# Sums kept between rounds are added by Pool, and the rounds are cut anew (one-core graph network)

## The chip, the cores and the metric

The kernel runs on one core of one Trainium2 chip. The number that counts is the device time of one launch in microseconds (us). The other seven cores are idle. Everything that is computed, the sorting of the edges into a count matrix included, happens inside that launch.

## What is computed

A graph network with 12,500 nodes of 64 features and 400,000 edges (src, dst). `src` is the node that receives, `dst` the node whose message is sent.

```python
h = relu(layernorm(x))
for l in range(3):
    mlp = lambda z: relu(z @ W1[l] + b1[l]) @ W2[l] + b2[l]
    msgs = mlp(h[dst])
    agg  = segment_sum(msgs, src, 12500)
    h    = mlp(h + agg)
out = x + h @ Wf + bf
```

Since the message depends on the sending node alone, the kernel computes one message for each node and forms `agg` as a product with a dense matrix of edge counts (12,544 x 12,544, four bits for each count).

## The kernel before, in words

**Counts.** The matrix is built once and kept in DRAM (`counts_dram`) as 98 tiles of 128 senders each. A build loop of 196 groups (`for k in range(BUILD * HG)`, index k, four groups for each pair of tiles) makes it. In a group VectorE (DVE) compares keys with two lists of numbers (`make_hots`, L752: 832 column elements, then 4,096 row elements); Pool multiplies the column half with the weights in place (`weigh`, L627); TensorE forms the counts of 32 columns of the group by 32 small matmuls (L1307, `multiply_group`); ScalarE packs the product (`keep_batch`, L1132); DVE transposes it two groups later (`turn_counts`, L760); and SyncE stores it (L439).

**Layer 0 beside the build.** `agg` is the sum over the 98 tiles of `parts` (messages as two 16-bit halves stacked to 128 columns) times counts, for 7 stretches of 1,792 nodes (SB = 7), each of four PSUM banks of 448 (SBB = 4). As the build goes on, this sum is made in rounds: a round takes 14 finished tiles (two chunks of CK = 7). So there are 7 rounds x 7 stretches = 49 units, and a unit is four banks with 14 matmuls each (L1336). DVE unpacks the counts of a unit in four steps, the low and the high nibbles of two chunks (`unpack_low`, L791; `unpack_high`, L799). Between two rounds a bank's sum is kept in SBUF (`kept_sums`): ScalarE copies it out of PSUM (L1141), and in the next round TensorE puts it back into PSUM with a float32 product with the identity (`add_kept`, L1331) ahead of the 14 matmuls.

One bank goes with each group from k = 32 on: 41 units (`FUSED`, 164 banks) lie inside the build loop. The last 8 units follow it, seven of them being the last round. There, unit by unit, DVE reads the finished sums, scales them and adds the rows of h (`read_sums`, L881 and L882, halves of 64 partitions), and TensorE runs the small network of the stretch before (`mlp_stage`) in between.

**Layers 1 and 2** read all counts again from DRAM, 14 chunks for each stretch (L1438, 28 matmuls for each chunk). They start when the scale of layer 1's messages is known (`find_peak`, Pool's `share_peak`, `make_scale`) and the first `parts` are rewritten.

**What sets the order.** Each engine runs its list in the order written, and semaphores tie the lists together. In a group DVE's list is: column compare, row compare, transposition of group k-2, one unpack step. TensorE's is: 32 small matmuls, (keys of the next pair), the kept sum, 14 matmuls. Pool's is: `weigh(k)`, and in every fourth group an indirect gather (L607).

## Time and profile before

| what | value |
|---|---|
| median of three runs | 2259.04 us (2255.1 to 2259.32) |
| the profiled execution's own time | 2256.61 us |
| its span | 2254.9 us |
| TensorE / DVE / ScalarE / Pool busy | 2096.7 / 1512.7 / 663.7 / 643.7 us |
| share of the span, in the same order | 93% / 67% / 29% / 29% |
| chain that ended last | TensorE 80%, DVE 13%, issue 4%, DMA 2% |
| float32 products of kept sums (L1331) | 83.2 + 83.1 us busy, 336 instructions |

The shares are means over stages that have different limits: a build stage up to about 945 us, the rest of layer 0 up to about 1104 us, and layers 1 and 2 after that. A row of the timeline begins with its start and its duration; an instruction's recorded duration can overlap that of the next one on the same engine, so the time which it takes from its engine is the distance from its start to the next start.

### The profile page before, as it was taken

The page shows a single profiled execution, that of the slowest core. Times are in us where ns is not written, and L with a number is a line of the kernel's source. Part 1 is how long each engine was busy: PE and PEld are TensorE (multiplying, and loading weights), DVE is VectorE, ACT ScalarE, POOL GpSimd, SP SyncE. Part 2 cuts the span into 40 slices and gives each one's busy share as a digit, 9 for nine tenths or more (in the row PEclk, how much of TensorE's full clock was granted, in tenths as well). Part 3 has the DMA queues.
Part 4 walks back from the last instruction along what each step waited for, and adds up shares of the span by engine and source line. Part 5 has one row for each costly group of instructions (what it writes and reads, how often), then busy time and mean ns, then how long its engine had stood idle before and what let it go on. Part 6 is the DMA issues. An engine that isn't in the chain of part 4 may idle for free.

```text
span 2254.9 us, 39446 instructions
## 1 busy us (share of the span) xinstructions
PE 2096.7 (93%) x15866; PEld 1153.6 (51%) x15866; DVE 1512.7 (67%) x1683; ACT 663.7 (29%) x1632; POOL 643.7 (29%) x287
## 2 busy tenths in 40 slices
PE   3566779999999999999997999999999999999998
PEld 3444445555555555545553555555555555555554
DVE  7899999999999999846645434444463443444344
ACT  4885655555555555411200000000010000000000
POOL 3666667777767776500000000000000000000000
PEclk8796999999999999999998999999999999999999
DMA  7256666666666666642343435444444554555552
GB/s 194 71 139 180 178 181 189 182 188 196 190 188 193 185 187 176 186 125 72 122 127 110 146 111 160 151 128 145 143 132 134 157 165 126 169 159 159 145 157 68
DMA packets 332824, 344.46 MB, mean 153 GB/s; under 512 B 21562, under 2 KB 303992, under 8 KB 332184
## 3 DMA queue, kind: packets, MB, share of 16 engines
q1 hardware_dynamic: 327516, 335.59, 50.6%
q0 software_dynamic: 2352, 6.43, 1.1%
q8 instruction: 94, 1.54, 0.3%
q10 hardware_dynamic: 2816, 0.53, 0.2%
q14 instruction: 46, 0.38, 0.0%
HBM read 252.58 MB, written 89.89 MB: 152 GB/s over the span
## 4 chain that ended last, share of the span: by engine, by line
PE 80%; DVE 13%; issue 4%; DMA 2%; SPq 0%; ACT 0%; POOL 0%; DVEq 0%; POOLq 0%
PE ps L1438 46%; PE ps L1336 18%; DVE arena L752 6%; PE ps L1331 5%; PE ps L1307 5%; PE ps L1400 2%; DVE arena L760 2%; PE ps L1392 2%; PE ps L1416 1%; DMA arena<-counts_dram 1%; DVE arena L791 1%; DVE arena L799 1%; DVE arena L725 1%; SPq L439 0%; DVE msg L778 0%
## 5 line engine op out<-in xcount | busy, mean ns | idle before, releaser
L1438 PE MATMUL ps<-arena,parts 128*128 128x448 fp8e4 x5488 | 1054.0, 353 | 11.9 <-DVE arena L882 11.9
L1438 PEld LDWEIGHTS ps<-arena,parts 128*128 128x128 f16 x5488 | 535.1, 98 | 531.4 <-issue 44.7
L627 POOL TENSOR_TENSOR arena<-arena,weight_now 128x416 int32<-128x416 int32 x196 | 540.8, 2759 | 274.0 <-DVE arena L752 273.3
L866 DVE TENSOR_SCALAR arena<-arena 128x3136 uint16<-128x3136 uint16 x196 | 191.5, 977 | 624.5 <-PE ps L1438 617.9
L1336 PE MATMUL ps<-arena,parts 128*128 128x448 fp8e4 x2744 | 554.9, 353 | 1.5 <-DVE parts L832 1.5
L752 DVE TENSOR_TENSOR arena<-row_iota,key_now 128x4096 f16<-128x4096 f16 x196 | 446.3, 2277 | 0.0
L1336 PEld LDWEIGHTS ps<-arena,parts 128*128 128x128 f16 x2744 | 267.1, 98 | 296.9 <-issue 83.1
L1132 ACT ACTIVATE arena<-ps 128x800 uint16<-128x800 f32 x392 | 332.3, 874 | 73.2 <-PE ps L1307 64.1
L1200 ACT ACTIVATE arena<-ps,b1s 128x448 f32<-128x448 f32 x42 | 26.6, 634 | 943.5 <-PE ps L1392 943.5
L1307 PE MATMUL ps<-arena 128*128 128x53 fp8e4 x6272 | 204.3, 189 | 79.8 <-DVE arena L752 41.2
L1307 PEld LDWEIGHTS ps<-arena 128*128 128x128 f16 x6272 | 187.7, 98 | 151.4 <-DVE arena L752 95.5
L619 POOL COPY hT<-arena 128x896 f32 (+1 forms) x14 | 13.2, 945 | 699.5 <-ACT arena L1209 699.5
L760 DVE STREAM_TRANSPOSE arena<-arena 128x800 int32<-128x800 int32 x196 | 195.2, 996 | 3.7 <-DMA counts_dram<-arena 3.7
L867 DVE TENSOR_SCALAR arena<-arena 128x3136 uint16<-128x3136 uint16 x196 | 190.0, 969 | 0.0
L647 POOL PARTITION_ALL_REDUCE good<-good x1 | 0.4, 409 | 526.8 <-DVE good L1000 526.8
L752 DVE TENSOR_TENSOR arena<-word_iota,key_now 128x832 uint16<-128x832 f16 x196 | 113.5, 579 | 4.6 <-ACT weight_now L1111 4.6
L1141 ACT ACTIVATE msg<-ps 128x448 f32<-128x448 f32 x84 | 45.7, 544 | 163.7 <-PE ps L1336 163.7
L1331 PE MATMUL ps<-msg,ident 128*128 128x448 f32 x168 | 83.2, 577 | 3.0 <-DVE arena L851 3.0
L1331 PE MATMUL ps<-arena,ident 128*128 128x448 f32 x168 | 83.1, 576 | 0.0
L1141 ACT ACTIVATE arena<-ps 128x448 f32<-128x448 f32 x84 | 45.7, 544 | 118.9 <-PE ps L1336 118.9
L607 POOL DMA_INDIRECT arena<-edges_dram,start_i x49 | 76.5, 1562 | 8.0 <-issue 3.5
L791 DVE TENSOR_SCALAR arena<-arena 128x3136 uint16<-128x3136 uint16 x82 | 76.2, 930 | 3.1 <-DMA arena<-counts_dram 3.0
(127 smaller groups left out, 1146.9 us busy)
## 6 DMA issues: line engine op xcount, KB each, us to landing
arena<-counts_dram SPq DMA_DIRECT2D x294, 784.0 KB, 4.6
counts_dram<-arena SPq DMA_DIRECT2D x784, 100.0 KB, 2.2
h_dram<-parts SPq DMA_DIRECT2D x2, 1536.0 KB, 7.2
edges_dram<-arena SPq DMA_DIRECT2D x2, 1400.0 KB
arena<-in_x_dram SPq DMA_DIRECT2D x14, 192.0 KB
out_dram<-arena SPq DMA_DIRECT2D x14, 192.0 KB
arena<-in_dst_dram SPq DMA_DIRECT2D x1, 1400.0 KB
arena<-in_src_dram SPq DMA_DIRECT2D x1, 1400.0 KB
```

The source lines that it names most:

```text
L627: nc.gpsimd.tensor_tensor(pairs, pairs, weight_now[:, h * HW:(h + 1) * HW].unsqueeze(2).to_broadcast([P, HW, WORDS // 2]), ALU.mult).then_ ...
L752: return v.tensor_tensor(out, numbers.rearrange("p (m two) -> p m two", two=2).unsqueeze(1).to_broadcast(shape), key.unsqueeze(2).to_broad ...
L760: v.transpose(ctile[:, k % 2, :].bitcast(I32), stage[:, k % 2, :].bitcast(I32)).then_inc(s["counts_turned"], 1)
L791: v.tensor_scalar(spread[:, n % WIDE, 0, :].bitcast(U16), ring0[:, n % RING0, :].bitcast(U16), 0x0F0F, None, ALU.bitwise_and).then_inc(s[" ...
L866: v.tensor_scalar(spread[:, c % WIDE, 0, :].bitcast(U16), packed, 0x0F0F, None, ALU.bitwise_and)
L867: v.tensor_scalar(spread[:, c % WIDE, 1, :].bitcast(U16), packed, 4, 0x0F0F, ALU.logical_shift_right, ALU.bitwise_and).then_inc(s["counts_ ...
L1132: a.activation(to, product(q)[:, :, 0:2 * LP].rearrange("p c (m two) -> p c m two", two=2), ACT.Copy, scale=1.0 / WEIGHT_UNIT)
L1141: a.activation(kept_sums(u % SB, b), ps[:, bank, 0:NB], ACT.Copy).then_inc(s["sums_kept"], 1)
L1307: last = t.matmul(product(q)[:, c, 0:COLS], hot_r[:, slot, w, :], hot_c8[:, slot, w, 0:COLS], start=True, stop=True)
L1331: t.matmul(ps[:, bank, 0:NB], ident[:], kept_sums(u % SB, b), start=True, stop=False)
L1336: last = t.matmul(ps[:, bank, 0:NB], parts[:, (ROUND * (u // SB) + c) * CK + k, :], spread[:, c, b // 2, at:at + NB].bitcast(F8), start=u ...
L1438: last = t.matmul(ps[:, b, 0:NB], parts[:, c * CK + k, :], spread[:, c % WIDE, b // 2, at:at + NB].bitcast(F8), start=start, stop=stop)
```

## The change

The kept sums no longer go back through TensorE. In the first round ScalarE copies the bank to `kept_sums`, already scaled; in later rounds it copies the bank, scaled, into one of two stages (`sums_stage`), and Pool adds the stage to `kept_sums` in SBUF (`add_sums`). Pool also adds the rows of h (`add_rows`), once for each of the 28 banks. `read_sums` of layer 0 becomes one operation over 128 partitions instead of two over 64.

There are eight rounds now, of 14, 14, 14, 14, 14, 12, 10 and 6 tiles, so 224 banks ("jobs"). `spread_jobs` gives each job of the first seven rounds the group with which it goes: none, one or two for each group. 179 jobs lie in the build loop, 17 kept ones and the 28 of the last round (six matmuls each) behind it. In the last round each bank is released and refilled by itself, and the steps of the small network go between banks. The scale of layer 1 is taken from the peaks of one stretch fewer and spread by TensorE instead of Pool. ScalarE turns the first keys ahead of the normalisation of the first rows. `row_edges` has 8-bit elements.

```diff
-ROUNDS = CH // ROUND
+COLUMNS = (7, 7, 7, 7, 7, 6, 5, 3)
+ROUNDS = len(COLUMNS)
+FROM = [sum(COLUMNS[:r]) for r in range(ROUNDS + 1)]
 UNITS = ROUNDS * SB
-AHEAD = KG + 1
-FUSED = BUILD - AHEAD
+JOBS = UNITS * SBB
+KEPT = JOBS - SB * SBB
+CREDIT = 16
 RING0 = 3
...
+def spread_jobs():
+    groups, credit = [], 0
+    for k in range(BUILD * HG):
+        credit = 2 * KG if len(groups) < SB * SBB else min(credit, 2 * KG) + CREDIT
+        while len(groups) < KEPT:
+            r = len(groups) // (SB * SBB)
+            if k < HG * (FROM[r + 1] + 1) or credit < 2 * COLUMNS[r]:
+                break
+            credit -= 2 * COLUMNS[r]
+            groups.append(k)
+    return groups + [BUILD * HG] * (JOBS - len(groups))
...
+JOB_GROUP = spread_jobs()
+IN_LOOP = JOB_GROUP.index(BUILD * HG)
+def jobs_with(k):
+    return [n for n in range(IN_LOOP) if JOB_GROUP[n] == k]
+def unpack_group(n):
+    return max(JOB_GROUP[n - 1] if n else 0, JOB_GROUP[n] - 1)
...
-EARLY_PEAKS = {1: 2 * (SB - 2), 2: 2 * (SB - 1)}
+EARLY_PEAKS = {1: 2 * (SB - 3), 2: 2 * (SB - 1)}
-        row_edges = sb("row_edges", [P, BUILD * QN, QW], F16)
+        row_edges = sb("row_edges", [P, BUILD * QN, QW], U8)
+        sums_stage = sb("sums_stage", [P, 2, NB], F32)
...
+            def add_sums(n):
+                pool.wait_ge(s["sums_kept"], n + 1)
+                to = kept_sums(n // SBB % SB, n % SBB)
+                nc.gpsimd.tensor_tensor(to, to, sums_stage[:, n % 2, :], ALU.add).then_inc(s["sums_added"], 1)
+            def add_rows(st, b):
+                own = slice(b // 2 * D, b // 2 * D + D)
+                to = kept_sums(st, b)[own]
+                nc.gpsimd.tensor_tensor(to, to, hT[own, st * SBH + b % 2 * NB:st * SBH + b % 2 * NB + NB],
+                                        ALU.add).then_inc(s["rows_added"], 1)
+            ODD_ROWS = HG * (BUILD - WR + 1)
             for k in range(BUILD * HG):
                 weigh(k)
+                for n in jobs_with(k - 1):
+                    if n >= SB * SBB:
+                        add_sums(n)
+                    elif n % SBB < 2:
+                        pool.wait_ge(s["sums_kept"], n + 1)
+                        add_rows(n // SBB, n % SBB)
+                if 0 <= k - ODD_ROWS < 2 * SB:
+                    n = k - ODD_ROWS
+                    if n == 0:
+                        for r in range(WR):
+                            pool.wait_ge(windows_gathered[r], 16 * len(range(r, WT, WR)))
+                    pool.wait_ge(s["hots_made"], k + 1)
+                    pool.wait_ge(s["sums_added"], max(m for m in jobs_with(k - 1) + [SB * SBB]) + 1 - SB * SBB)
+                    add_rows(n // 2, 2 + n % 2)
+                    pool.wait_ge(s["rows_added"], 2 * SB + n + 1)
                 if k % HG == 2 and k // HG + WR < WT:
                     gather(k // HG + WR)
-            with pool.Fori(0, SB - 2) as i:
+            for n in jobs_with(BUILD * HG - 1):
+                add_sums(n)
+            for n in range(IN_LOOP, KEPT):
+                add_sums(n)
...
+            def unpack_step(n):
+                u, c = n // SBB, n % ROUND
+                m = u * ROUND + c
+                size = tiles_of(u, c)[1] * SBH
+                packed = ring0[:, m % RING0, 0:size].bitcast(U16)
+                if n % SBB < 2:
+                    dve.wait_ge(round_loaded[m % RING0], 16 * (m // RING0 + 1))
+                    if u:
+                        dve.wait_ge(s["sums_done"], SBB * (u - 1) + 2)
+                    v.tensor_scalar(spread[:, c, 0, 0:size].bitcast(U16), packed, 0x0F0F, None, ALU.bitwise_and).then_inc(
+                        s["low_unpacked"], 1)
+                else:
+                    if u:
+                        dve.wait_ge(s["sums_done"], SBB * u)
+                    v.tensor_scalar(spread[:, c, 1, 0:size].bitcast(U16), packed, 4, 0x0F0F, ALU.logical_shift_right,
+                                    ALU.bitwise_and).then_inc(s["counts_unpacked"], 1)
...
+                    if l == 0:
+                        if i == 0 and b == 0:
+                            dve.wait_ge(s["sums_added"], KEPT - SB * SBB)
+                            dve.wait_ge(s["rows_added"], SB * SBB)
+                        if i:
+                            dve.wait_ge(s["u_done"], 2 * (i - 1) + b % 2 + 1)
+                        v.scalar_tensor_tensor(zP[:, b * NB:(b + 1) * NB], ps[:, b, 0:NB], scal[:, 0, 6:7], kept_sums(i, b),
+                                               ALU.mult, ALU.add).then_inc(s["sums_read"], 1)
+                        continue
...
-            act.wait_ge(s["variance_made"], 1)
-            a.activation(stat[:, 2, :], stat[:, 1, :], ACT.Sqrt).then_inc(s["root_made"], 1)
...
             relate_rows(0)
             keep_keys(0, 0)
             keep_keys(0, 1)
+            act.wait_ge(s["variance_made"], 1)
+            a.activation(stat[:, 2, :], stat[:, 1, :], ACT.Sqrt).then_inc(s["root_made"], 1)
+            act.wait_ge(s["norm_made"], 1)
+            make_h0(0)
...
+            def keep_sums(n):
+                u, b = n // SBB, n % SBB
+                act.wait_ge(s["sums_done"], n + 1)
+                if u < SB:
+                    if b < 2:
+                        act.wait_ge(s["parts_made"], ROUND * (u + 1))
+                    to = kept_sums(u, b)
+                else:
+                    if n >= SB * SBB + 2:
+                        act.wait_ge(s["sums_added"], n - 1 - SB * SBB)
+                    to = sums_stage[:, n % 2, :]
+                a.activation(to, ps[:, b % 2, 0:NB], ACT.Copy, scale=scal[:, 0, 6:7]).then_inc(s["sums_kept"], 1)
             def upper_parts(l, n):
...
-            def add_kept(u, b, bank):
-                t.matmul(ps[:, bank, 0:NB], ident[:], kept_sums(u % SB, b), start=True, stop=False)
+            def add_bank(n):
+                u, b = n // SBB, n % SBB
+                bank = b if n >= KEPT else b % 2
+                if n % (SB * SBB) == 0:
+                    pe.wait_ge(s["parts_made"], -(-2 * FROM[u // SB + 1] // CK))
+                if n < 2:
+                    pe.wait_ge(s["hidden0_kept"], BLOCKS)
+                elif n < KEPT:
+                    pe.wait_ge(s["sums_kept"], n - 1)
+                elif n < KEPT + 2:
+                    pe.wait_ge(s["sums_kept"], KEPT)
+                elif n == KEPT + 2:
+                    pe.wait_ge(s["scale_made"], 1)
+                elif n == KEPT + 3:
+                    pe.wait_ge(s["keys_kept"], 2 * BUILD)
                 else:
-                    pe.wait_ge(s["hidden0_kept"], BLOCKS)
-                if u >= SB:
-                    add_kept(u, b, b % 2)
+                    pe.wait_ge(s["sums_read"], n - KEPT - SBB + 1)
                 for c in range(ROUND):
+                    first, tiles = tiles_of(u, c)
                     pe.wait_ge(s["low_unpacked" if b < 2 else "counts_unpacked"], ROUND * u + c + 1)
-                    last = multiply_chunk(u, c, b, b % 2, c == ROUND - 1)
+                    for k in range(tiles):
+                        at = k * SBH + b % 2 * NB
+                        last = t.matmul(ps[:, bank, 0:NB], parts[:, first + k, :], spread[:, c, b // 2, at:at + NB].bitcast(F8),
+                                        start=c == 0 and k == 0, stop=c == ROUND - 1 and k == tiles - 1)
...
+            MLP_AT = ((0, 1), (2,), (3,), (4, 5))
+            for n in range(IN_LOOP, JOBS):
+                add_bank(n)
+                i, b = n // SBB - (UNITS - SB), n % SBB
+                if i >= 1:
+                    for stage_n in MLP_AT[b]:
+                        mlp_stage(0, i - 1, stage_n)
+                if i == SB - 1 and b == 0:
+                    turn_peak(1)
+                if i == SB - 1 and b == 1:
+                    spread_peak(1)
```

The order of Pool's list late in the build loop, before (`weigh` is `arena<-arena,weight_now`, the DMA is the gather):

```order
L627 TENSOR_TENSOR arena<-arena,weight_now 128x32x13 x4
L607 DMA arena<-edges_dram,start_i 128x256
L627 TENSOR_TENSOR arena<-arena,weight_now 128x32x13 x4
L607 DMA arena<-edges_dram,start_i 128x256
L627 TENSOR_TENSOR arena<-arena,weight_now 128x32x13 x4
```

Nothing but the gather stands between the multiplies. And now, at the same place (the new operation reads `sums_stage`; half of the kept sums lie in `msg`, half in `arena`):

```order
L669 TENSOR_TENSOR arena<-arena,weight_now 128x32x13
L679 TENSOR_TENSOR arena<-arena,sums_stage 128x448
L669 TENSOR_TENSOR arena<-arena,weight_now 128x32x13
L679 TENSOR_TENSOR msg<-msg,sums_stage 128x448
L669 TENSOR_TENSOR arena<-arena,weight_now 128x32x13
L679 TENSOR_TENSOR msg<-msg,sums_stage 128x448
L669 TENSOR_TENSOR arena<-arena,weight_now 128x32x13
L679 TENSOR_TENSOR arena<-arena,sums_stage 128x448 x2
L649 DMA arena<-edges_dram,start_i 128x256
L669 TENSOR_TENSOR arena<-arena,weight_now 128x32x13
```

Where four multiplies followed each other between two gathers, an addition of 128x448 stands behind each, in some groups two. In the whole list 148 such additions and 28 of 64x448 (with `hT`) stand ahead of the last multiply, and 20 additions behind it.

DVE's list late in the build loop, before (L760 transposes, L799 and L791 unpack):

```order
L752 TENSOR_TENSOR arena<-word_iota,key_now 128x32x26
L752 TENSOR_TENSOR arena<-row_iota,key_now 128x4096
L760 STREAM_TRANSPOSE arena<-arena 128x800
L799 TENSOR_SCALAR arena<-arena 128x3136
L752 TENSOR_TENSOR arena<-word_iota,key_now 128x32x26
L752 TENSOR_TENSOR arena<-row_iota,key_now 128x4096
L760 STREAM_TRANSPOSE arena<-arena 128x800
L799 TENSOR_SCALAR arena<-arena 128x3136
```

Each group has the same four pieces. And now, two groups of the second to fourth round (L833 transposes, L868 and L873 unpack):

```order
L833 STREAM_TRANSPOSE arena<-arena 128x800
L873 TENSOR_SCALAR arena<-arena 128x3136
L825 TENSOR_TENSOR arena<-word_iota,key_now 128x32x26
L825 TENSOR_TENSOR arena<-row_iota,key_now 128x4096
L833 STREAM_TRANSPOSE arena<-arena 128x800
L873 TENSOR_SCALAR arena<-arena 128x3136
L868 TENSOR_SCALAR arena<-arena 128x3136
```

The pieces of a group are the same; now and then a group has a second unpack step. Ahead of the last row compare stand 164 unpack steps of 3,136 elements before, and 140 of 3,136, 28 of 2,688 and 11 of 2,240 now.

TensorE's list in the last round, one stretch, before (L1331 is the kept sum, L1392, L1400 and L1416 are the small network):

```order
L1336 MATMUL ps<-arena,parts 128x448 x7
L1331 MATMUL ps<-msg,ident 128x448
L1336 MATMUL ps<-arena,parts 128x448 x7
L1392 MATMUL ps<-arena,W1s 64x448 x2
L1331 MATMUL ps<-msg,ident 128x448
L1336 MATMUL ps<-arena,parts 128x448 x7
L1392 MATMUL ps<-arena,W1s 64x448 x2
L1331 MATMUL ps<-arena,ident 128x448
L1336 MATMUL ps<-arena,parts 128x448 x7
L1400 MATMUL ps<-arena,W2b 128x448 x2
L1331 MATMUL ps<-arena,ident 128x448
L1336 MATMUL ps<-arena,parts 128x448 x14
```

Each bank begins with its kept sum, and its 14 matmuls stand in two halves of 7. And now (L1431 is the banks' product; L1477, L1485 and L1501 are the small network):

```order
L1431 MATMUL ps<-arena,parts 128x448 x210
L1477 MATMUL ps<-arena,W1s 64x448 x4
L1431 MATMUL ps<-arena,parts 128x448 x6
L1485 MATMUL ps<-arena,W2b 128x448 x2
L1431 MATMUL ps<-arena,parts 128x448 x6
L1485 MATMUL ps<-arena,W1b 128x448 x2
L1431 MATMUL ps<-arena,parts 128x448 x6
L1501 MATMUL ps<-W2b,arena 128x128 x7
```

The four float32 products of a stretch are gone, and a bank is 6 matmuls where it was 14. The 210 matmuls of the first row are 10 of the build loop's last job, 17 x 10 of the kept jobs behind the loop, and 5 x 6 of the last round's first five banks.

## Rows read from the trace of the kernel before

**Rows 1.** Busy time by window: columns are us, each engine's busy us (instructions), clock, DMA.

```profile
100.00:150.00 50.00, 29.85 (x476) 24.71 (x475) 49.73 (x48) 44.89 (x124) 34.52 (x15) 0.90 0.54 137
...
250.00:300.00 50.00, 38.47 (x476) 22.33 (x473) 50.00 (x47) 30.69 (x76) 35.54 (x14) 1.00 0.67 191
...
800.00:850.00 50.00, 49.97 (x542) 28.29 (x541) 50.00 (x45) 29.61 (x75) 34.75 (x14) 1.00 0.63 183
```

**Rows 2.** Timeline, one build group on DVE, TensorE and Pool: start us, us, engine, line, operation.

```profile
799.39 2.27 DVE L752 TENSOR_TENSOR arena<-row_iota,key_now 128x4096 f16<-128x4096 f16 x1
...
799.72 2.81 PE L1336 MATMUL ps<-arena,parts 128*128 128x448 fp8e4 x14
...
799.82 2.61 POOL L627 TENSOR_TENSOR arena<-arena,weight_now 128x416 int32<-128x416 int32 x1
...
801.59 0.99 DVE L760 STREAM_TRANSPOSE arena<-arena 128x800 int32<-128x800 int32 x1
...
802.52 0.92 DVE L791 TENSOR_SCALAR arena<-arena 128x3136 uint16<-128x3136 uint16 x1
...
802.53 0.99 PE L1307 MATMUL ps<-arena 128*128 128x53 fp8e4 x32
...
803.36 1.00 PE L1331 MATMUL ps<-arena,ident 128*128 128x448 f32 x2
...
803.38 0.57 DVE L752 TENSOR_TENSOR arena<-word_iota,key_now 128x832 uint16<-128x832 f16 x1
...
803.87 2.27 DVE L752 TENSOR_TENSOR arena<-row_iota,key_now 128x4096 f16<-128x4096 f16 x1
...
804.20 2.81 PE L1336 MATMUL ps<-arena,parts 128*128 128x448 fp8e4 x14
```

**Rows 3.** Groups by form, the banks' product and Pool's row copy: busy us, mean ns.

```profile
L1336 PE MATMUL ps<-arena,parts 128*128 128x448 fp8e4 x2744 | 554.9, 353 | 1.5 <-DVE parts L832 1.5
...
L619 POOL COPY hT<-arena 128x896 f32 x11 | 10.3, 933 | 618.2 <-ACT arena L1209 618.2
```

**Rows 4.** Timeline, the first two build groups, DVE and Pool.

```profile
63.57 0.59 DVE L752 TENSOR_TENSOR arena<-word_iota,key_now 128x832 uint16<-128x832 f16 x1 [4.64 <-ACT weight_now L1111]
...
64.08 2.28 DVE L752 TENSOR_TENSOR arena<-row_iota,key_now 128x4096 f16<-128x4096 f16 x1
...
64.32 2.80 POOL L627 TENSOR_TENSOR arena<-arena,weight_now 128x416 int32<-128x416 int32 x1 [10.12 <-DVE arena L752]
...
66.28 1.29 DVE L752 TENSOR_TENSOR arena<-word_iota,key_now 128x832 uint16<-128x832 f16 x1
```

**Rows 5.** Timeline, a group whose multiply was issued late behind a gather.

```profile
195.45 2.28 DVE L752 TENSOR_TENSOR arena<-row_iota,key_now 128x4096 f16<-128x4096 f16 x1
...
196.39 2.10 POOL L627 TENSOR_TENSOR arena<-arena,weight_now 128x416 int32<-128x416 int32 x1
```

**Rows 6.** Line 627 by itself: duration ns min/median/max, first and last start us.

```profile
L627 POOL TENSOR_TENSOR arena<-arena,weight_now x196: 2097/2821/2830, 64.3 to 943.1; 128x416 int32<-128x416 int32 x196
```

**Rows 7.** Timeline of the set-up, DVE integer passes beside a Pool cast.

```profile
30.45 0.99 DVE L700 TENSOR_SCALAR arena<-arena 125x1600 int32<-125x1600 int32 x1
...
30.59 2.21 POOL L596 CAST arena<-hT 125x1600 f16<-125x1600 int32 x1 [5.41 <-DVE hT L699]
...
31.35 2.31 DVE L701 TENSOR_SCALAR arena<-arena 125x1600 int32<-125x1600 int32 x1
```

**Rows 8.** Timeline of the last round: its begin, two save_h copies, layer 1's first matmuls.

```profile
942.86 2.27 DVE L752 TENSOR_TENSOR arena<-row_iota,key_now 128x4096 f16<-128x4096 f16 x1
...
953.47 1.11 PE L1331 MATMUL ps<-msg,ident 128*128 128x448 f32 x1 [2.99 <-DVE arena L851]
...
1013.49 0.93 POOL L619 COPY hT<-arena 128x896 f32 x1 [19.43 <-ACT arena L1209]
...
1033.86 0.93 POOL L619 COPY hT<-arena 128x896 f32 x1 [19.43 <-ACT arena L1209]
...
1104.39 0.92 PE L1438 MATMUL ps<-arena,parts 128*128 128x448 fp8e4 x4
```

233 lines of the change are left out of this document (86 added, 147 removed).

## The prediction

> **What bounds the kernel now.** I read the windows first. Late in the build loop TensorE is busy 49.97 of 50 us and DVE 50.00 of 50 [rows 1], so the totals of the page (93% and 67%) can't say which of the two sets the pace. The timeline of one group does [rows 2]. The reader is to see distances from start to start: on DVE the row compare holds its engine from 799.39 to 801.59 (2.20 us), the transposition to 802.52 (0.93), the unpack step to 803.38 (0.86), the column compare to 803.87 (0.49). That is 4.48 us with no gap. TensorE: 14 matmuls and what stands behind them up to 802.53 (2.81), 32 small matmuls up to 803.36 (0.83), the kept sum up to 804.20 (0.84), again 4.48. But 14 matmuls need only 14 x 0.189 = 2.65 us (the row of 14 lasts 2.81 and one lasts 0.353 by its mean [rows 3], so 13 distances are 2.46 us, 0.189 each), and the small matmuls begin just after Pool's multiply ends (799.82 + 2.61 = 802.43). So TensorE has little room, and DVE none: the build loop is DVE's, TensorE being 0.2 us behind it. Behind the loop it is the other way: no key compares are left and TensorE works through the last round.
>
> **Pool's multiply tells most for this change.** Pool is busy 2.61 us on it, but it ends at 802.43, that is 0.77 us after the row compare ends (799.39 + 2.27 = 801.66). A multiply that was issued 0.94 us after its row compare's start takes 2.10 us and ends at 198.49, again 0.76 after the compare's end at 197.73 [rows 5]; the usual one takes 2.82 [rows 6]. The work is thus about 0.75 us, and the rest is waiting until DVE's two-input compare is through. It goes the other way as well. In the first groups there is no transposition between the row compare and the next column compare: the column compare at 66.28 takes 1.29 us where it takes 0.57 elsewhere [rows 2, 4], 0.72 more, and ends 0.45 us after the multiply (64.32 + 2.80 = 67.12). In the set-up a one-input integer pass of DVE takes 2.31 us beside Pool's cast where the one before it takes 0.99 [rows 7]. So on this chip, for these forms, the one waits for the other in full. The Trainium skill, "SBUF — State Buffer", section on the shared port pair, says the same as a rule: a DVE instruction in a two-port mode, or with two SBUF inputs against a Pool instruction that reads SBUF, excludes Pool for its whole length, and the reverse. The rule speaks against this change, and the rows bear it out.
>
> **The change part by part.**
>
> 1. *Kept sums off TensorE, in the loop.* 84 + 84 banks lose a float32 product (336 instructions, two for each) of 0.84 us each [rows 2]. In the loop (164 banks, 136 of them from the second round on) that frees 136 x 0.84 = 114 us of TensorE. It lies beside DVE, which sets 4.48 us without it, so I count it at nothing. If DVE were faster it would be worth something; DVE gets more to do.
>
> 2. *More of layer 0 inside the loop.* 179 unpack steps instead of 164: 140 at 0.86; 28 of 2,688 elements at 0.86 x 6/7 = 0.74; 11 of 2,240 at 0.61. That is 120.4 + 20.7 + 6.7 = 147.8 against 164 x 0.86 = 141.0: **+7 us** on DVE.
>
> 3. *Pool's additions in the loop.* 148 of 128x448 and 28 of 64x448 (per partition as long): 176. Each stands behind a multiply. In a group DVE leaves one piece that doesn't shut out Pool, the transposition, 0.93 us, and the multiply already fills 0.72 to 0.77 of it. The addition then runs into the unpack step, or, if its bank is copied late, into the column compare, or it waits for the next transposition and pushes the multiply over its end. In each case what Pool needs beyond 0.93 us is taken from DVE. No row shows a float32 addition on Pool. From the multiply (832 elements read in 0.72) I get 896/832 x 0.72 = 0.78 us; the copy of 896 elements, as many reads, takes 0.933 [rows 3]. With 0.78 the price is 0.72 + 0.78 - 0.93 = 0.57; with 0.93 and nothing covered it is 0.93. Below, the bound is 0 (the addition isn't shut out and shuts nothing out), since nothing here could make DVE faster. I take 0.70, nearer to the multiply's row (it is the operation of the same kind), with 0.1 for the change from one Pool instruction to the next: 176 x 0.70 = **+123 us**. Ends for the range: 100 and 164.
> The Trainium skill, "GPSIMD Engine Reference", section on elementwise cycle accounting, gives about 2.6 cycles of 1.2 GHz for an element of a two-input addition. As an estimate from that page 448 elements are 0.97 us, and the sum would come out some 11 us higher than mine, inside my range.
> Behind Pool's addition stands the next multiply, and TensorE's small matmuls wait for that; they have a group's time of room, and DVE's compares wait for matmuls two groups back. ScalarE copies each bank with the old duration and waits for the addition two jobs back, which is through by then.
>
> 4. *The last round.* Before, from the last row compare's start at 942.86 (end 945.13) to layer 1's first matmul at 1104.39 are 159.3 us [rows 8]. It adds up: 8.3 us until 953.47 (a last group, then counts stored and loaded again); 8 units x 56 x 0.189 = 84.7; 32 kept sums x 0.84 = 26.9; the small network six times. One stretch is 1033.86 - 1013.49 = 20.37 us, less 56 x 0.189 = 10.6 and 4 x 0.84 = 3.4, leaves 6.4 us for it, six times 38.6. Sum 158.5. After: 8.3 + (17 x 10 + 28 x 6) x 0.189 = 63.9, no kept sums, 38.6: 110.8. **-48 us**. A stretch is then 4.5 + 6.4 = 10.9 us; DVE has four reads in it instead of eight, and four unpack steps of 1,344 elements (0.86 x 3/7 = 0.37 us) instead of four of 3,136, so I let TensorE lead. The copies of the small network on ScalarE lie beside six matmuls (1.13 us) instead of 14: up to 1 us a stretch could come back, 6 us in all. The 20 additions behind the loop go beside 1.9 us jobs and cost nothing.
>
> 5. *Head.* DVE waits 4.64 us for the first keys at 63.57 [rows 4], since ScalarE makes eight rows of h first. That order is turned: **-4.6 us** at best, and 0 if these rows are then missed in the first groups.
>
> 6. *Scale of layer 1, the wider `read_sums`, 8-bit `row_edges`*: beside TensorE's last banks, before and after; nothing, within 3 us either way.
>
> **The sum**, against the profiled execution's own 2256.6 us: + 7 + 123 - 48 - 4.6 = 2334. Median of the runs before is 2259.0, 2.4 above that execution and inside their own scatter of 4; I say 2335.
>
> **The rivals.**
>
> *A, the additions cost DVE nothing.* Then the change does what its parts suggest: 2256.6 + 7 - 48 - 4.6 = **2211**. For it: Pool has 15 of 50 us unused in [rows 1], and if its busy time is what it seems an addition finds room. Against: that busy time is mostly waiting, and three separate rows show DVE held. 14%.
>
> *B, middle.* Only additions that meet an unpack step or a compare by chance cost something, about half of them at 0.57: 50 us, total 2261, no change. It needs a DVE with gaps; there are none. 4%.
>
> *C, TensorE's clock.* With the kept sums gone TensorE works (2.65 + 0.83) of about 5.2 us in a group, 67%. At 60% busy, part of it at the lower clock, the granted clock was 0.90 [rows 1]. If it stayed at the lower of its two levels (1.2 GHz) in the loop, a group would need 7 us of TensorE and the loop would be TensorE's: 164 x (7.0 - 4.5) = 410 us, 2620; over a quarter of the loop it is 60 to 100 us on top of mine, 2400 to 2440. Against: at 77% busy (38.47 of 50) it was 1.00. 6%.
>
> *D, the addition is slow by itself*, over 1.2 us: 176 x 1.05 = 185, 2396. From a price of 0.22 us on, the additions eat up the 45 us that the rest saves; that is the point from which the change turns from faster to slower. 10%.
>
> My own case has 66%. Slower by over 0.2% (about what a measurement of this kernel can tell from no change) holds mine, C and D: 0.82; the same 0.04; faster 0.14. For the likeliest case alone the range is 2305 to 2378; the one I give, 2290 to 2395, takes in most of D and leaves A and C out.
>
> **What would show it.** Right: in the build loop a group with an addition takes about 5.2 us, in a group without one 3.6; unpack steps or column compares of DVE are 1.5 us or so long instead of 0.92 or 0.57, and DVE is still 50 of 50 busy; TensorE falls to about 35 of 50 there. The last row compare starts near 1068 us instead of 943, and from there to layer 1 are about 111 us; layers 1 and 2 keep their time. Wrong: unpack steps at 0.92 us with additions beside them (A), a clock of 0.5 (C), additions over 1.2 us long with no row compare above them (D). If the last round takes over 120 us, step 4 has missed a wait.

## The result and the profile after

The changed kernel takes **2385.23 us** (median of 4 runs, 2382.60 to 2386.91), the kernel before 2258.92 us in the same comparison (4 runs, 2255.10 to 2259.32). The ratio is 1.0562, with a 95% interval of 1.0544 to 1.0580: 5.6% slower. The forecast was 2335 us, slower with a chance of 0.82, and a range of 2290 to 2395. Direction and range held; the loss is +126 us where +76 was forecast.

Four moments split a profiled execution into stretches that can be compared: the start of row compare 32 (the first round has its groups behind it), the start of the last row compare, the start of layer 1's first matmul, and the end of the span. They come from DVE's timeline and from the lines of the row compare and of layer 1's product. Stretches in us:

| kernel | to compare 32 | compare 32 to the last | last compare to layer 1 | layer 1 to the end | span |
|---|---|---|---|---|---|
| before | 199.9 | 742.9 | 161.5 | 1150.5 | 2254.9 |
| after | 195.7 | 915.0 | 118.3 | 1151.7 | 2380.8 |
| difference | -4.2 | +172.1 | -43.2 | +1.2 | +125.9 |

The forecast had +130 us for the loop, -48 for the last round and -4.6 for the head. So of the 48.5 us by which the sum was too low 42 are in the build loop. Its last row compare and the first matmul of layer 1 stand in the rows of the two lines, of the kernel after (duration ns as min/median/max, then first and last start); before they were at 942.86 and 1104.39 [rows 8]:

```profile
L825 DVE TENSOR_TENSOR arena<-row_iota,key_now x196: 2272/2279/3227, 58.3 to 1110.8; 128x4096 f16<-128x4096 f16 x196
```

```profile
L1523 PE MATMUL ps<-arena,parts x5488: 352/352/581, 1229.1 to 2365.9; 128*128 128x448 fp8e4 x196
```

The windows late in the loop (columns as in [rows 1]) show who sets the pace:

```profile
700.00:750.00 50.00, 38.12 (x436) 22.13 (x435) 50.00 (x38) 24.47 (x57) 39.48 (x21) 0.93 0.59 159
800.00:850.00 50.00, 36.62 (x411) 21.29 (x407) 49.20 (x37) 25.47 (x62) 36.94 (x20) 0.91 0.60 172
```

TensorE went from 49.97 us of 50 to between 36.6 and 38.1, DVE is still at 49.2 to 50.0, but with 37 or 38 instructions instead of 45. The same engine does fewer pieces in the same time: pieces became longer. The timeline of one group of the kernel after shows which (start us, us, engine, line; to be held against [rows 2]):

```profile
705.95 2.28 DVE L825 TENSOR_TENSOR arena<-row_iota,key_now 128x4096 f16<-128x4096 f16 x1
...
706.17 2.82 POOL L669 TENSOR_TENSOR arena<-arena,weight_now 128x416 int32<-128x416 int32 x1 [0.59 <-DVE arena L825]
...
708.15 1.00 DVE L833 STREAM_TRANSPOSE arena<-arena 128x800 int32<-128x800 int32 x1
708.95 1.13 POOL L679 TENSOR_TENSOR arena<-arena,sums_stage 128x448 f32<-128x448 f32 x1
...
709.08 1.83 DVE L868 TENSOR_SCALAR arena<-arena 128x3136 uint16<-128x3136 uint16 x1
...
710.83 0.58 DVE L825 TENSOR_TENSOR arena<-word_iota,key_now 128x832 uint16<-128x832 f16 x1
...
711.34 2.28 DVE L825 TENSOR_TENSOR arena<-row_iota,key_now 128x4096 f16<-128x4096 f16 x1
```

The group is 711.34 - 705.95 = 5.39 us instead of 4.48. Pool's addition begins at 708.95, as soon as the multiply is through, inside the transposition; that ends at about 709.1 and isn't held. The unpack step that follows ends at 710.9, 0.8 us after the addition's end (708.95 + 1.13 = 710.08), and one that nothing holds up lasts 0.92. So it did its work only when the addition was over: 1.83 instead of 0.92, all of the 0.91 that the group grew.

### The profile page after: what moved, and what is told of

The parts are those of the page before. It is cut to its first block, busy times and chain, and to the rows that moved or that the text cites. A ratio compares the mean times of both kernels' runs of the same rounds, so it can differ in the third digit from the quotient of the medians.

```text
span 2380.8 us, 39405 instructions
## 1 busy us (share of the span) xinstructions
PE 2013.3 (85%) x15534; PEld 1122.9 (47%) x15534; DVE 1664.6 (70%) x1684; ACT 697.5 (29%) x1660; POOL 875.6 (37%) x482
## 4 chain that ended last, share of the span: by engine, by line
PE 56%; DVE 29%; issue 8%; DMA 3%; SPq 1%; POOL 1%; ACT 1%; DVEq 0%; POOLq 0%; ACTq 0%
PE ps L1523 44%; DVE arena L825 13%; PE ps L1431 6%; DVE arena L833 5%; DVE arena L873 4%; DVE arena L868 3%; PE ps L1485 2%; DMA counts_dram<-arena 2%; PE ps L1477 2%; PE ps L1386 1%; SPq L487 1%; PE ps L1501 1%; DMA arena<-counts_dram 1%; DVE arena L798 1%; POOL arena L669 0%
## 5 line engine op out<-in xcount | busy, mean ns | idle before, releaser
L1523 PE MATMUL ps<-arena,parts 128*128 128x448 fp8e4 x5488 | 1055.1, 353 | 15.5 <-DVE arena L958 11.9
L933 DVE TENSOR_SCALAR arena<-arena 128x3136 uint16<-128x3136 uint16 x196 | 191.5, 977 | 621.8 <-PE ps L1523 621.3
L669 POOL TENSOR_TENSOR arena<-arena,weight_now 128x416 int32<-128x416 int32 x196 | 517.7, 2642 | 215.8 <-DVE arena L825 214.7
L1431 PE MATMUL ps<-arena,parts 128*128 128x448 fp8e4 x2744 | 584.1, 368 | 4.0 <-DVE parts L910 1.7
L1386 PE MATMUL ps<-arena 128*128 128x53 fp8e4 x6272 | 219.8, 194 | 296.4 <-DVE arena L825 205.6
L1431 PEld LDWEIGHTS ps<-arena,parts 128*128 128x128 f16 x2744 | 267.8, 101 | 258.3 <-issue 52.3
L1386 PEld LDWEIGHTS ps<-arena 128*128 128x128 f16 x6272 | 203.4, 101 | 365.8 <-DVE arena L825 311.5
L661 POOL COPY hT<-arena 128x896 f32 (+1 forms) x14 | 13.1, 938 | 633.2 <-ACT arena L1288 633.2
L833 DVE STREAM_TRANSPOSE arena<-arena 128x800 int32<-128x800 int32 x196 | 196.0, 1000 | 2.7 <-DMA counts_dram<-arena 2.6
L934 DVE TENSOR_SCALAR arena<-arena 128x3136 uint16<-128x3136 uint16 x196 | 190.2, 970 | 0.0
L1223 ACT ACTIVATE sums_stage<-ps,scal 128x448 f32<-128x448 f32 x168 | 106.6, 634 | 209.8 <-PE ps L1431 209.8
L873 DVE TENSOR_SCALAR arena<-arena 128x3136 uint16<-128x3136 uint16 (+3 forms) x112 | 157.2, 1417 | 6.8 <-PE ps L1431 6.8
L825 DVE TENSOR_TENSOR arena<-word_iota,key_now 128x832 uint16<-128x832 f16 x196 | 154.9, 790 | 0.0
L868 DVE TENSOR_SCALAR arena<-arena 128x3136 uint16<-128x3136 uint16 (+3 forms) x112 | 143.3, 1292 | 15.2 <-PE ps L1431 9.3
L679 POOL TENSOR_TENSOR arena<-arena,sums_stage 128x448 f32<-128x448 f32 x84 | 113.5, 1353 | 14.1 <-ACT sums_stage L1223 13.4
L679 POOL TENSOR_TENSOR msg<-msg,sums_stage 128x448 f32<-128x448 f32 x84 | 110.7, 1318 | 14.8 <-ACT sums_stage L1223 14.7
```

The source lines that it names most:

```text
L669: nc.gpsimd.tensor_tensor(pairs, pairs, weight_now[:, h * HW:(h + 1) * HW].unsqueeze(2).to_broadcast([P, HW, WORDS // 2]), ALU.mult).then_ ...
L679: nc.gpsimd.tensor_tensor(to, to, sums_stage[:, n % 2, :], ALU.add).then_inc(s["sums_added"], 1)
L825: return v.tensor_tensor(out, numbers.rearrange("p (m two) -> p m two", two=2).unsqueeze(1).to_broadcast(shape), key.unsqueeze(2).to_broad ...
L833: v.transpose(ctile[:, k % 2, :].bitcast(I32), stage[:, k % 2, :].bitcast(I32)).then_inc(s["counts_turned"], 1)
L868: v.tensor_scalar(spread[:, c, 0, 0:size].bitcast(U16), packed, 0x0F0F, None, ALU.bitwise_and).then_inc(s["low_unpacked"], 1)
L873: v.tensor_scalar(spread[:, c, 1, 0:size].bitcast(U16), packed, 4, 0x0F0F, ALU.logical_shift_right, ALU.bitwise_and).then_inc(s["counts_un ...
```

## The experiments

In each row below the median and the ratio are against runs of the kernel before on the same chip (2257.99 to 2259.82 us in all of them). The last two columns are the loop and the last round as defined above, from the run's own trace.

| kernel | median us | ratio (95%) | loop | last round |
|---|---|---|---|---|
| e1_add8 | 2238.34 | 0.9906 (0.9890 to 0.9923) | 770.4 | 117.7 |
| e2_add224 | 2302.06 | 1.0198 (1.0181 to 1.0215) | 835.2 | 117.4 |
| e3_copy | 2301.38 | 1.0196 (1.0179 to 1.0213) | 831.5 | 118.0 |
| e4_before_pool_adds | 2398.29 | 1.0624 (1.0607 to 1.0642) | 886.3 | 159.2 |
| e8_no_adds | 2233.52 | 0.9888 (0.9872 to 0.9905) | 766.2 | 117.6 |
| e12_no_adds_gather_first | 2223.31 | 0.9842 (0.9826 to 0.9859) | 754.4 | 118.1 |
| e13_gather_first | 2403.60 | 1.0637 (1.0619 to 1.0654) | 936.1 | 118.4 |
| e9_before_memsets | 2287.53 | 1.0122 (1.0105 to 1.0139) | 776.4 | 160.2 |
| e10_before_head | 2255.12 | 0.9981 (0.9971 to 0.9990) | 746.1 | 163.6 |
| e5_te_sums | 2268.34 | 1.0037 (1.0023 to 1.0052) | 787.0 | 131.3 |
| e7_split | 2256.21 | 0.9988 (0.9978 to 0.9998) | 786.3 | 118.5 |
| e11_split_c14 | 2234.19 | 0.9894 (0.9877 to 0.9911) | 739.9 | 141.0 |

An instruction is called held below where it lasts longer than elsewhere because the other engine's is not through. The theory was that DVE's pieces wait for Pool's additions (their cost is the length of the additions), the rival that the loss is in what else the change did: more unpack steps, ScalarE's waits for the two stages, gathers that are issued later.

**The additions shortened, all else left.** e1 adds 8 columns of each bank, e2 half of it:

```diff
-nc.gpsimd.tensor_tensor(to, to, sums_stage[:, n % 2, :], ALU.add).then_inc(s["sums_added"], 1)
+nc.gpsimd.tensor_tensor(to[:, 0:8], to[:, 0:8], sums_stage[:, n % 2, 0:8], ALU.add).then_inc(s["sums_added"], 1)
```

(The 28 additions of `hT` likewise; 0:224 in e2. In the columns that aren't added the sums lack the rounds between the first and the last.)

> The changed kernel, with each of Pool's additions cut to 8 of its 448 elements per partition (so 440 of 448 sums keep only their first round, and most rows of h are left out). Number, order and waits of the additions are unchanged. Theory (DVE and Pool exclude each other for as long as an addition lasts): from the first job on the 164 groups take 172 us longer than before, 7 of it for more unpack steps, so 176 additions cost 0.94 us each; with the length gone almost all of that goes: 2385 - 165 = 2220, up to 2240 if starting an instruction costs something. Rival 1 (the waits and the number of Pool's instructions cost the time): 2385, no change. Rival 2 (the new placement of jobs and TensorE's lower clock cost it): 2385 too. In the profile the theory wants unpack steps of 0.92 us beside the additions.

> The same with additions of 224 of the 448 elements (half of each sum is left out). An addition lasts 1.07 us beyond the multiply before it in the profile of the changed kernel, of which about 0.1 is start. Theory: half its length gives back about 0.5 us for each of 176, 2385 - 88 = 2297, on a line between 448 and 8 elements (2385 and 2220 give 2302). Rivals (number, waits, placement): 2385. If DVE won the contest whenever the addition is short enough to fit in the transposition, the time would lie on a bend: near 2230.

e1 took 2238.34 us: 147 us of the kernel after's 2385 hang on the number of columns added. Order, count, waits and stages are all the same in e1, so the rival that put the loss there is out. e2 took 2302.06, on the line between 8 and 448 columns, which gives 2238.3 + 216/440 x 146.9 = 2310 at 224; it is 8 us below it. The one point between shows no sign of a cost that comes in steps, by whole pieces of DVE.

**One input fewer.** e3 copies the stage where the kernel adds it (the sum is left out):

```diff
-nc.gpsimd.tensor_tensor(to, to, sums_stage[:, n % 2, :], ALU.add).then_inc(s["sums_added"], 1)
+nc.gpsimd.tensor_copy(to, sums_stage[:, n % 2, :]).then_inc(s["sums_added"], 1)
```

> The changed kernel, with the 168 additions of stages replaced by copies of the stage over the kept sum (448 elements, one operand read instead of two, so earlier rounds are left out of the sums); the 28 additions of rows of h stay. Theory, reads set the length: a copy of 448 takes about half of an addition (a copy of 896 took 0.93 us with start), 0.45 to 0.5 us less for each of the 148 in the loop: 2385 - 70 = 2315. If length is set by elements written and not by reads, 2385. If copies don't hold DVE up at all: 2385 - 148 x 0.94 = 2246.

2301.38, below the 2315 expected. Its timeline, one group:

```profile
804.01 1.00 DVE L833 STREAM_TRANSPOSE arena<-arena 128x800 int32<-128x800 int32 x1
804.79 0.56 POOL L679 COPY arena<-sums_stage 128x448 f32<-128x448 f32 x1
...
804.94 1.24 DVE L868 TENSOR_SCALAR arena<-arena 128x3136 uint16<-128x3136 uint16 x1
```

The copy takes 0.56 us, half of the addition's 1.13, and the unpack step 1.24 instead of 1.83. The difference of DVE's piece (0.59) is that of Pool's piece (0.57). Behind a multiply that leaves the last 0.2 us of the transposition, DVE pays what sticks out.

**The additions alone, in the kernel before.** e4 takes none of the change, and puts one addition of the same size, whose result nobody uses, behind each multiply from that of group k = 33 on:

```diff
+if k > HG * AHEAD:
...
+    nc.gpsimd.tensor_tensor(uS[:, 0:NB], hT[:, 0:NB], hT[:, NB:2 * NB], ALU.add).then_inc(s["extra_added"], 1)
```

> The kernel before, with nothing of the change but one extra addition on Pool of 128x448 float32 behind each multiply from group 33 on (163 of them, two reads of hT, written to a buffer that is no longer used; each waits for the one before it). Nothing waits for them, and TensorE, DVE and ScalarE keep their lists. Theory: each takes 0.94 us from DVE as in the changed kernel: 2259 + 153 = 2412 (2385 to 2425). Rival (Pool has room, and the time comes from the new schedule or from the kept sums' new path): 2259.

2398.29, inside the 2385 to 2425 of the theory and 139 us from the rival's number. Its group, and the rows of the addition and of one unpack line (busy us, mean ns of one):

```profile
801.29 1.00 DVE L767 STREAM_TRANSPOSE arena<-arena 128x800 int32<-128x800 int32 x1
802.09 1.13 POOL L640 TENSOR_TENSOR uS<-hT 128x448 f32<-128x448 f32 x1
...
802.22 1.84 DVE L806 TENSOR_SCALAR arena<-arena 128x3136 uint16<-128x3136 uint16 x1
```

```profile
L640 POOL TENSOR_TENSOR uS<-hT 128x448 f32<-128x448 f32 x163 | 184.3, 1131 | 0.0
L806 DVE TENSOR_SCALAR arena<-arena 128x3136 uint16<-128x3136 uint16 x82 | 150.6, 1837 | 0.0
```

The picture is the kernel after's, within 0.01 us, though no other engine waits for the addition here. The median rose by 140 us (from 2257.99) for 163 additions, 0.86 each, and 162 of the loop's unpack steps are over 1.3 us long. And the granted clock of TensorE was 1.00 in the window of 800 to 850 us, where the kernel after had 0.91:

```profile
800.00:850.00 50.00, 42.04 (x446) 23.41 (x444) 50.00 (x38) 23.85 (x58) 40.61 (x22) 1.00 0.59 172
```

The same price at both clocks: rival C, TensorE's clock, has no visible part in it.

**No additions at all, and the gathers.** e8 takes Pool's additions out of the kernel after, leaving its waits and signals (the sums of the rounds between the first and the last and the rows of h are left out); e12 takes e8 and issues the gather directly behind the multiply, not behind the additions and their waits.

```diff
-nc.gpsimd.tensor_tensor(to, to, sums_stage[:, n % 2, :], ALU.add).then_inc(s["sums_added"], 1)
+pool.sem_inc(s["sums_added"], 1)
```

(The 28 additions of `hT` likewise.)

> The changed kernel with all 196 Pool additions replaced by a bare count of their semaphores (the sums keep only the first and the last round, and the rows of h are left out). Theory: DVE is free of them, so the build loop falls back to 7 us over the kernel before, plus what the new placement costs: 2385 - 165 = 2220. With 8 elements the same kernel took 2238; if starting an instruction holds DVE about 0.1 us (176 of them) this run is at 2220, and if the 18 us come from the placement (groups without a job, pairs of jobs, lower TensorE clock) it stays at 2238. Rival (waits): 2385.

> The changed kernel without additions (as before, the semaphores are only counted), and with the gather placed straight behind the multiply of its group instead of behind the waits for the kept sums. Theory: in the run without additions 30 unpack steps of DVE still lasted up to 1.77 us, since Pool stood waiting for a kept sum, then issued the gather late (1.92 us), and so the next multiply missed the transposition and met the unpack step; that is worth 16 us of the 22 by which that run lay above my 2211. Then 2233.5 - 16 = 2217. Rival (groups without a job and the lower clock make the 22 us): 2233.

e8 took 2233.52, e12 2223.31: of the 16 us that e12 was to give, 10 came. With e8 the loop's loss can be booked by DVE's lines. From compare 32 to the last, the kernel after (busy us, mean ns of one; three forms of each unpack line):

```profile
L825 DVE TENSOR_TENSOR arena<-row_iota,key_now 128x4096 f16<-128x4096 f16 x164 | 386.9, 2359 | 0.0
L825 DVE TENSOR_TENSOR arena<-word_iota,key_now 128x832 uint16<-128x832 f16 x164 | 135.3, 825 | 0.0
L873 DVE TENSOR_SCALAR arena<-arena 128x3136 uint16<-128x3136 uint16 x70 | 118.9, 1699 | 0.0
...
L868 DVE TENSOR_SCALAR arena<-arena 128x3136 uint16<-128x3136 uint16 x69 | 93.6, 1366 | 4.8 <-DMA arena<-counts_dram 4.8
...
L868 DVE TENSOR_SCALAR arena<-arena 128x2688 uint16<-128x2688 uint16 x14 | 22.3, 1592 | 0.0
...
L873 DVE TENSOR_SCALAR arena<-arena 128x2688 uint16<-128x2688 uint16 x14 | 17.4, 1283 | 0.0
L868 DVE TENSOR_SCALAR arena<-arena 128x2240 uint16<-128x2240 uint16 x6 | 8.7, 1455 | 0.0
L873 DVE TENSOR_SCALAR arena<-arena 128x2240 uint16<-128x2240 uint16 x5 | 7.2, 1456 | 0.0
```

and e8 in the same stretch (two of its six unpack groups are shown):

```profile
L824 DVE TENSOR_TENSOR arena<-row_iota,key_now 128x4096 f16<-128x4096 f16 x164 | 373.8, 2280 | 0.0
...
L824 DVE TENSOR_TENSOR arena<-word_iota,key_now 128x832 uint16<-128x832 f16 x164 | 96.0, 586 | 0.0
L872 DVE TENSOR_SCALAR arena<-arena 128x3136 uint16<-128x3136 uint16 x70 | 69.3, 990 | 0.0
L867 DVE TENSOR_SCALAR arena<-arena 128x3136 uint16<-128x3136 uint16 x69 | 68.2, 998 | 7.4 <-DMA arena<-counts_dram 7.4
```

All unpack steps together are 268.1 us after and 169.3 in e8: +98.8. Column compares: +39.3. Row compares: +13.1. Sum 151.2, for a difference of the two loops of 915.0 - 766.2 = 148.8 us. Two thirds of that difference is paid by the unpack step, a quarter by the column compare, the rest by the row compare.

e8 also shows why a late gather costs. The multiply of this group had to wait for one:

```profile
402.17 1.92 POOL L649 DMA_INDIRECT arena<-edges_dram,start_i  x1 [2.64 <-ACT sums_stage L1222]
403.17 1.00 DVE L832 STREAM_TRANSPOSE arena<-arena 128x800 int32<-128x800 int32 x1
404.10 1.77 DVE L872 TENSOR_SCALAR arena<-arena 128x3136 uint16<-128x3136 uint16 x1
404.11 0.91 POOL L669 TENSOR_TENSOR arena<-arena,weight_now 128x416 int32<-128x416 int32 x1
```

Pool waited 2.64 us for ScalarE's copy, the gather then ran until 404.09, almost to the end of the transposition (404.17), and the multiply (0.91 us, which is all of its work) fell on the unpack step, which took 1.77. In e8 12 unpack steps of the loop are over 1.3 us long, in e12 none, and its loop is 11.8 us shorter. e12 is thus the run in which next to nothing of Pool holds DVE: against it the loop of the kernel after is 160.6 us longer, 0.91 for each of 176 additions, the same 0.91 as in the group above.

**Is the early gather worth as much with the additions?** e13 makes e12's move in the kernel after itself.

> The changed kernel with nothing but the gather moved in the same way. Theory: the additions keep costing 0.86 us each (from the 140 us of 163 in the kernel before), only the late gathers' part goes: 2385 - 14 = 2371. If the additions already hide the late gathers, 2385.

2403.60: a miss for both numbers expected, 18 us slower than the kernel after. The timeline says why (its first row is two unpack steps in one):

```profile
701.01 1.81 DVE L868 TENSOR_SCALAR arena<-arena 128x3136 uint16<-128x3136 uint16 x2
...
701.08 1.87 POOL L649 DMA_INDIRECT arena<-edges_dram,start_i  x1 [0.15 <-issue]
702.75 1.82 DVE L825 TENSOR_TENSOR arena<-word_iota,key_now 128x832 uint16<-128x832 f16 x1
702.97 1.14 POOL L679 TENSOR_TENSOR arena<-arena,sums_stage 128x448 f32<-128x448 f32 x1
```

The gather now fills the place behind the multiply, the addition comes later and falls on the column compare (1.82 us instead of 0.58: 1.24 lost, where the unpack step loses 0.91). The greater part of the loss is another, at the row compare:

```profile
724.84 1.71 POOL L649 DMA_INDIRECT arena<-edges_dram,start_i  x1
...
726.13 4.58 DVE L825 TENSOR_TENSOR arena<-row_iota,key_now 128x4096 f16<-128x4096 f16 x1
...
726.57 1.14 POOL L679 TENSOR_TENSOR arena<-arena,sums_stage 128x448 f32<-128x448 f32 x1
...
727.65 0.90 POOL L669 TENSOR_TENSOR arena<-arena,weight_now 128x416 int32<-128x416 int32 x1
```

The row compare starts while the gather still runs, and ends 2.16 us after the multiply (730.71 against 728.55). The addition and the multiply both went ahead of it, though its record begins before theirs, and it lasts 4.58 us instead of 2.28. 19 row compares of the loop are over 4.5 us long, none in the kernel after (its longest is 3.23). Over the loop the unpack steps are 42 us shorter than in the kernel after, the row compares 51 and the column compares 12 longer. An addition costs least directly behind the multiply, where part of it lies under the transposition.

**A Pool instruction that reads nothing.** e9 is e4 with `nc.gpsimd.memset(uS[:, 0:NB], 0.0)` in place of the addition.

> The kernel before with 163 extra Pool memsets of 128x448 float32 (written, nothing read) in the place where the extra additions stood, which cost 140 us, 0.86 each. A memset of 384 takes 0.42 us in the set-up. If length alone counts, the multiply (0.72) and a memset (0.35 to 0.42) overrun the transposition (0.93) by 0.14 to 0.2 and the start by 0.1: 2259 + 163 x 0.3 = 2305. If a Pool instruction that only writes doesn't shut out DVE's unpack step, 2259. The Trainium skill, SBUF - State Buffer, says that a two-port pass of DVE (the unpack step) is shut out by any Pool access, and a two-input one only by reads: by it 2259 to 2305.

2287.53, +28 us, 0.17 each (in its trace the loop is 33.5 us longer, 0.21 each). Its rows (mean ns last):

```profile
L806 DVE TENSOR_SCALAR arena<-arena 128x3136 uint16<-128x3136 uint16 x82 | 94.3, 1150 | 0.0
...
L640 POOL MEMSET uS<- 128x448 f32 x163 | 76.2, 467 | 0.0
```

The memset of 0.47 us holds the unpack step by 0.23 (1.15 instead of 0.92). So the unpack step is shut out even by a Pool instruction that reads no SBUF. The Trainium skill, "SBUF — State Buffer", section "Who interferes with whom", has this difference: a DVE operation with two SBUF inputs contends only with Pool instructions that read, one in a two-port mode with any. The run agrees for the unpack step, with 0.23 us; whether a row compare lets a memset pass wasn't tried.

**The head alone.** e10 turns, in the kernel before, ScalarE's order at the start (keys and rows first, `make_h0(0)` behind them).

> The kernel before with only ScalarE's head changed as in the changed kernel: the first keys ahead of the square root and the first rows of h. Theory: DVE's 4.64 us of waiting go and the first groups keep most of it (in the changed kernel the 33rd group began 4.2 us earlier): 2259 - 4 = 2255. Rival: the first messages come late and take it back: 2259.

2255.12, ratio 0.9981 (0.9971 to 0.9990), which is -4.3 us: the forecast's -4.6 at best.

**Could the saving be had without the price?** e5 keeps the rest of the change and returns the sums through TensorE, one float32 product a bank, in the loop and behind it. e7 does so only in the loop, and has Pool add the 17 banks behind it.

```diff
+if u < SB:
+    at = u * SBH + b % 2 * NB
+    t.matmul(ps[:, bank, 0:NB], rows_ident[:, b // 2, :], hT[:, at:at + NB], start=True, stop=False)
+elif n < IN_LOOP:
+    t.matmul(ps[:, bank, 0:NB], ident[:], kept_sums(u % SB, b), start=True, stop=False)
```

(`n < KEPT` in e5. ScalarE copies to `kept_sums`, without Pool.)

> The change without Pool: eight rounds, the new placement, the last round bank by bank and the head as in the changed kernel, but the kept sums of rounds 2 to 7 go back through TensorE as before, the rows of h are added by TensorE in the first round (28 float32 products with a scaled identity), and DVE adds the kept sum in the last round as in the changed kernel. Theory: no unpack step is held up; the loop is TensorE's and DVE's together (0.83 + 9/8 x 3.49 us a group for TensorE, 4.8), some 20 us longer than before, the last round 8.3 + 17 x 2.73 + 31.8 + 38.6 + 4 = 129 us instead of 158.5, head -4: 2245 (2235 to 2262). Rival (the new placement itself costs the time): 2350 or more.

> As the kernel with TensorE's kept sums, but the 17 kept jobs behind the build loop are added by Pool from two stages, where DVE isn't the bound. Theory: Pool's additions are free behind the loop and take 17 float32 products of 0.84 us off TensorE: 14 us less than that kernel, 2231 (2220 to 2248), faster than the kernel before and than the changed one. Rival (Pool's additions cost wherever they stand): 15 us more than that kernel, 2260.

Both missed in level: 2268.34 and 2256.21 where 2245 and 2231 were expected. Between them lie 12 us (14 expected): behind the loop, where DVE isn't the bound, Pool's additions cost next to nothing (the last round is 12.8 us shorter, of 14.3 that 17 products of 0.84 take). The level is TensorE's: 179 jobs stand in the loop of both where 164 did before, each with its float32 product, and the window of 800 to 850 us shows TensorE full and DVE not, in e7:

```profile
800.00:850.00 50.00, 50.00 (x518) 29.43 (x517) 47.29 (x44) 26.92 (x67) 31.98 (x14) 1.00 0.66 186
```

I had read in [rows 2] that TensorE had no more than 0.2 us of room in a group, and forgot it in this expectation. e11 is e7 with 168 jobs in the loop and 28 behind it (`CREDIT` 14 instead of 16).

> The kernel with TensorE's kept sums in the loop and Pool's behind it, with credit 14 instead of 16: 168 jobs in the loop, one for each group up to the sixth round, and 28 behind it, all 28 added by Pool. Theory: with 179 jobs TensorE (0.83 + 3.49 a job) became the bound of the loop (groups of 4.8 to 5.0 us, 786 us for 164 groups against 743). With one job a group it needs 4.44 against DVE's 4.48: about 750. Behind it 8.3 + 28 x 1.89 + 31.8 + 38.6 + 4 = 136 against 161: 2257 - 4 + 7 - 25 = 2235 (2228 to 2248). Rival (TensorE's work is the same wherever it stands): 2256.

2234.19, on the number expected, and the same window has both engines full again:

```profile
800.00:850.00 50.00, 49.59 (x540) 28.17 (x539) 50.00 (x46) 29.35 (x73) 35.16 (x14) 1.00 0.62 173
```

Against the kernel before that is 1.06% less (0.9877 to 0.9911), with all of the computation kept: loop 739.9 instead of 742.9, last round 141.0 instead of 161.5. It is 6.3% below the kernel after.

## Why the prediction came out as it did

**Step 3, the additions, is where it failed: a size, not the mechanism.** The mechanism (Pool and DVE exclude each other, and what Pool needs beyond the transposition is taken from DVE) is shown by e1, e4 and e8. The term was 176 x 0.70 = 123 us. Measured, e12 against the kernel after: 160.6 / 176 = 0.91 each, 38 us more. Against e8 it is 148.8 / 176 = 0.845, 26 us more, but e8 still loses 11.8 us to late gathers. The forecast's likeliest case, with a range of its own of 2305 to 2378, missed 2385; the range given held by the room that it left for rival D. Two sizes in the term were off. The addition itself: I sized it by the multiply, 0.78 us with 0.1 for the change from one to the next; it is 1.13 us long. Directly behind a multiply only about 0.2 of the 1.13 is covered, which leaves the 0.91 lost in each group of the timelines. And my upper end, 0.93, was not an upper end: an addition at the column compare costs up to 1.24 (e13). The Trainium skill's price ("GPSIMD Engine Reference", elementwise cycle accounting, 0.97 us as estimated in the forecast) was the better size, though still below the 1.13 measured. The 11 us that the forecast adds for it leave out the 0.1 that my own term has: with it they are 0.86 each and 28 us. Two operations of the same kind, both `TENSOR_TENSOR` on Pool, don't cost the same per element: the int32 multiply of 416 is through in 0.91 [e8's timeline], the float32 addition of 448 in 1.13.

**Waits of Pool, which the forecast left at nothing.** "Behind Pool's addition stands the next multiply", I wrote, and counted room for it. But the gather stands there too, and it stands behind a wait for ScalarE's copy. In e8 that pushes multiplies out of the transposition's place: 11.8 us (against e12). In the kernel after itself it is less: by its timeline 10 pieces of DVE are held by a multiply alone, 7 us in all, and 166 by additions, three of these by a multiply as well. With the additions in place the early gather even loses time (e13). So 148.8 and 11.8 are one way to cut up the 160.6 us, not two prices that hold by themselves. Each instruction behind an added wait has to be counted.

**Steps 1 and 2.** Taking the kept sums off TensorE bought nothing in the loop, as said: e12, without any addition and with early gathers, still has 754.4 us there where before had 742.9. Of the difference of 11.5, 7.5 are the longer list of unpack steps (146.9 instead of 139.4 us, from each start to the next), forecast as 7. Another 3.7 are DVE's waits for counts that come back from DRAM: 3.1 us in the loop of before, 6.8 in that of e12 (why they grew is open). In these two rows the wait stands behind the second bar:

```profile
L791 DVE TENSOR_SCALAR arena<-arena 128x3136 uint16<-128x3136 uint16 x81 | 75.3, 930 | 3.1 <-DMA arena<-counts_dram 3.0
```

```profile
L867 DVE TENSOR_SCALAR arena<-arena 128x3136 uint16<-128x3136 uint16 x69 | 64.3, 943 | 6.8 <-DMA arena<-counts_dram 6.8
```

The loop's sum is 11.5 + 11.8 + 148.8 = 172.1.

**Step 4.** From the end of the last row compare (1110.8 + 2.3 = 1113.1) to layer 1's first matmul are 116.0 us, 110.8 forecast (159.3 before, counted likewise from the compare's end, which my text called its start). A stretch is 11.5 us, not 10.9 (Pool's copies of h begin at 1163.25 and 1220.60, five stretches: 11.47), the "up to 1 us a stretch" that I had named: 3.4 us. And at the end TensorE waits for DVE:

```profile
1226.51 1.87 DVE L910 SCALAR_TENSOR_TENSOR parts<-msg,scal,parts 128x448 f16<-128x448 f32 x3
1228.30 1.27 DVE L948 SCALAR_TENSOR_TENSOR arena<-ps,scal,msg 128x448 f32<-128x448 f32 x2
1229.12 2.40 PE L1523 MATMUL ps<-arena,parts 128*128 128x448 fp8e4 x6 [3.62 <-DVE arena L948]
```

It is 3.62 us; by the timeline the wider `read_sums` of the last stretch (L948) stands behind the scale, the parts and the first unpack steps in DVE's list. Step 6 had put that beside TensorE's last banks. No run moved it. The two make 7.0 us, of which the rest of the stretch made up 1.8.

**Step 5.** Head -4.2 in the kernel after and -4.7 in e10's trace (compare 32 starts at 195.2 instead of 199.9); forecast -4.6.

**The rivals.** A (additions free, 2211): e8 and e12, which have none, give 2233.5 and 2223.3, so A's number wasn't to be had even then, and the additions cost 149 to 161 us on top. B: in the loop of the kernel after 116 unpack steps are over 1.3 us long, 44 column compares over 1.2 and 15 row compares over 2.9, together 175 for 176 additions (12, 2 and none in e8), so it is no chance meeting. C: the clock fell, to 0.91 and 0.93 in the two windows, and no cost of it is to be seen, as DVE was busy for 49.2 us of 50 or more; e4 pays the same at 1.00. D (an addition over 1.2 us) is wrong by a little, with 1.13, but its total of 2396 is nearer than mine. That is partly luck: its 185 us for the additions are 24 more than the 160.6 measured, and 11 us that stand elsewhere make up for part of that.

**What was to be seen.** Groups of 5.39 us (5.2 said), unpack steps of 1.83 and column compares of 1.53 (1.5 said), DVE at 49 to 50 of 50, TensorE at 37 to 38. The last compare started at 1110.8, not 1068. "A group without an addition 3.6" was a slip of mine: it contradicts the 4.48 of [rows 2], and e8 has 766.2 / 164 = 4.67. The price from which the change turns slower was another: 45.6 / 176 is 0.26 us, not 0.22. It changes nothing in the sum.

**The sum as measured**: head -4.2, loop +172.1, last round -43.2, layers 1 and 2 +1.2, together +125.9 against a difference of the spans of 2380.8 - 2254.9 = 125.9.
